# Attention with each head of a pair on its own 64 rows of the array, in packed banks

## What is computed

```python
q = (x @ wq).reshape(B, T, 32, 16); k = x @ wk; v = x @ wv
scores = einsum('bqhd,bkd->bhqk', q, k) / 4, causal
out = softmax(scores) @ v, heads side by side, @ wo
h = linear8bit(xn, W1, b1); g = silu(linear8bit(h, W2, b2))
return x + out * g
```

## Time and profile before

| | us |
|---|---|
| median of 3 runs | 799.04 (798.92 to 799.80) |
| profiled execution | 802.84, span 801.1 |
| PE busy | 764.9 (95%) |
| DVE busy | 638.7 (80%) |
| ACT busy | 402.7 (50%) |
| POOL busy | 257.6 (32%) |
| preparation | 0 to 81.3 |
| attention | 81.3 to 408.6 |
| the rest | 408.7 to 801.1 |

### The profile page before, as it was taken

The page is one execution under the profiler, slowest core; times in us unless marked ns, Lnnn a source line. Parts: engine busy times, 40 slices in busy tenths (PEclk is TensorE's granted clock), DMA queues, the critical chain, the costliest instruction groups (busy, mean ns, idle before and its releaser), DMA issues. The chain is left out here.

```text
span 801.1 us, 12089 instructions
## 1 busy us (share of the span) xinstructions
PE 764.9 (95%) x4253; PEld 579.5 (72%) x4253; DVE 638.7 (80%) x1094; ACT 402.7 (50%) x683; POOL 257.6 (32%) x335
## 2 busy tenths in 40 slices
PE   4999999999999999999999999999997999999995
PEld 3877665556676666775578888788886788888884
DVE  7988989999999899995537476666658998599957
ACT  3454166767677676777634554544553333122212
POOL 7313135555555555554621110110100000036504
PEclk9999589999999999999999999999999999999998
DMA  7421303333322223334554444222013778536982
GB/s 258 153 106 53 86 11 91 82 80 92 90 81 83 82 81 95 89 113 123 161 192 159 143 158 144 81 78 79 27 47 97 251 220 259 164 106 219 334 287 105
DMA packets 58348, 103.37 MB, mean 129 GB/s; under 512 B 8480, under 2 KB 16688, under 8 KB 56752
## 3 DMA queue, kind: packets, MB, share of 16 engines
q1 hardware_dynamic: 58288, 102.60, 40.3%
HBM read 52.76 MB, written 36.70 MB: 112 GB/s over the span
## 5 line engine op out<-in xcount | busy, mean ns | idle before, releaser
L914 DVE TENSOR_REDUCE rowmax<-ps 128x2 f32<-128x512 f32 (+3 forms) x384 | 210.9, 591 | 20.7 <-PE ps L991 18.8
L835 ACT ACTIVATE probs<-ps 128x512 f32<-128x512 f32 (+1 forms) x352 | 175.2, 557 | 72.4 <-PE ps L1004 70.7
L991 PE MATMUL ps<-km,stack 128*128 128x256 f32 (+3 forms) x512 | 151.0, 350 | 2.0 <-PEq L187 1.9
L1004 PE MATMUL ps<-stack,ks 128*128 128x512 f32 (+1 forms) x352 | 133.1, 388 | 2.6 <-ACT probs L835 2.6
L991 PEld LDWEIGHTS ps<-km,stack 128*128 128x128 f32 (+1 forms) x512 | 96.0, 201 | 42.2 <-DVE rowmax L914 22.5
L817 POOL TENSOR_SCALAR_AFFINE_SELECT probs<-probs 128x512 f32<-128x512 f32 x128 | 81.0, 641 | 79.1 <-ACT probs L835 77.6
L1806 PE MATMUL ps<-big_h 128*128 128x512 f32 x256 | 100.4, 392 | 2.4 <-issue 2.0
L1808 PE MATMUL ps<-big_h,big_l 128*128 128x512 f32 x256 | 100.3, 392 | 0.0
L1807 PE MATMUL ps<-big_l,big_h 128*128 128x512 f32 x256 | 100.2, 391 | 0.0
L1017 PE MATMUL ps<-probs,vones 128*32 128x512 f32 (+3 forms) x1024 | 82.2, 439 | 0.2 <-POOL probs L817 0.2
L1004 PEld LDWEIGHTS ps<-stack,ks 128*128 128x128 f32 x352 | 67.5, 192 | 11.9 <-ACT probs L835 6.3
(11 more groups left out here) (227 smaller groups left out, 1384.3 us busy)
## 6 DMA issues: line engine op xcount, KB each, us to landing
stack<-big_h SPq DMA_DIRECT2D x128, 64.0 KB, 2.0
h_scratch<-hs SPq DMA_DIRECT2D x7, 1024.0 KB, 4.5
hload<-h_scratch SPq DMA_DIRECT2D x14, 512.0 KB, 5.4
xn_scratch<-xa SPq DMA_DIRECT2D x4, 1024.0 KB, 4.4
stack<-big_l SPq DMA_DIRECT2D x64, 64.0 KB, 2.0
xi<-xn_scratch SPq DMA_DIRECT2D x16, 256.0 KB, 2.8
xe_scratch<-xm SPq DMA_DIRECT2D x16, 256.0 KB, 2.3
w2n<-in_L_ffn_W_dram SPq DMA_DIRECT2D x4, 1024.0 KB, 6.7
```

Of the source, the lines that this page charges most:

```text
L835: nc.scalar.activation(probs[p][:, o:o + nh * w], ps[:, STB[n % NST], 0:nh * w], ACT.Exp).then_inc(s_exp, 1)
L914: nc.vector.tensor_reduce(dst, src, AX_X, ALU.max).then_inc(s_red, 1)
L991: last = nc.tensor.matmul(dst, stack[u % 3][rows, hp, P * qt:P * (qt + 1)], km[rows, u // KT, p0:p0 + npar, keys], start=True, stop=True)
L1004: ins = nc.tensor.matmul(ps[:, STB[n % NST], 0:nh * w].rearrange("p (h q) -> p h q", h=nh), ks[:, u // KT, p, P * kt:P * (kt + 1)], stack[ ...
```

## The change

A head of a pair now has its own 64 rows of the stack: 48 rows of queries (high, low, high), two rows for the maximum, and a staircase of 14 rows with ten steps each (steps of 2^12). The keys need only one version each. What was a piece of two heads is now two products on rows 0-63 and 64-127, issued one after the other into two banks, and all banks are filled to 512 columns: 20 banks of maxima and 20 of scores per unit instead of 24 and 22, CH = 20, LAG = 10. The steps of everything else move along. A unit's queries are 24 DMAs of 16 rows, its maxima two DMAs. The values product of key tile 3 moves into the first group. The projection's rows are permuted by loading wo with eight DMAs. SP waits for the spare rows of a stack before the queries' DMAs, and no longer before the maxima's. POOL fills whole stacks, and adds the staircase to the keys. The wait for the last stores of projected rows moves from f = 1 to f = 0.

```diff
-SPARE, RUN, STEP = 100, 5, 2.0 ** 25
+SPARE, RUN, STEP, OWN = 50, 10, 2.0 ** 12, 32.0
...
-        km = sa("km", [P, B, 2, T], F32R)
-        ks = sa("ks", [P, B, 2, T], F32R)
+        km = sa("km", [P, B, T], F32R)
+        ks = sa("ks", [P, B, T], F32R)
...
+        HALF_ROWS, KEPT = P // 2, 3 * HD
         def fill_spare(i):
-            spare = slice(6 * HD, P)
-            return nc.gpsimd.tensor_copy(stack[i][spare, :, :].rearrange("r h (j k) -> r (h j) k", k=P),
-                                         later_q[spare, :].rearrange("r (o k) -> r o k", o=1)
-                                         .broadcast_to([P - 6 * HD, NPAIR * QT, P]))
+            return nc.gpsimd.tensor_copy(stack[i][:, :, :].rearrange("r h (j k) -> r (h j) k", k=P),
+                                         later_q[:, :].rearrange("r (o k) -> r o k", o=1)
+                                         .broadcast_to([P, NPAIR * QT, P]))
...
             for hp in range(NPAIR):
-                src = slice(2 * HD * hp, 2 * HD * (hp + 1))
-                for n, part in enumerate((big_h, big_l, big_h)):
-                    sp.dma_start(stack[u % 3][2 * HD * n:2 * HD * (n + 1), hp, :].bitcast(F32),
-                                 part[src, f, tok].bitcast(F32)).then_inc(s_sq[u % 3][hp], 16)
+                for a in range(2):
+                    src = slice(HD * (2 * hp + a), HD * (2 * hp + a + 1))
+                    for n, part in enumerate((big_h, big_l, big_h)):
+                        lo = HALF_ROWS * a + HD * n
+                        sp.dma_start(stack[u % 3][lo:lo + HD, hp, :].bitcast(F32),
+                                     part[src, f, tok].bitcast(F32)).then_inc(s_sq[u % 3][hp], 16)
...
-                            sp.dma_start(wo_in, wo.rearrange("(k p) n -> p k n", p=P)).then_inc(s_wload["wo"], 16)
+                            wo_rows = wo.rearrange("(k p) n -> p k n", p=P)
+                            for h2, h1, a in itertools.product(range(2), repeat=3):
+                                to, of = 2 * HD * (2 * h1 + a) + HD * h2, 2 * HD * (2 * h2 + h1) + HD * a
+                                sp.dma_start(wo_in[to:to + HD], wo_rows[of:of + HD]).then_inc(s_wload["wo"], 16)
...
+                        sp.wait_ge(s_z, 1)
                         stack_queries(sp, 0)
...
-                steps_along(later_k, [-STEP ** t for t in range(RUN + 1)])
                 fill_spare(0).then_inc(s_z, 1)
                 pool.wait_ge(s_z, 1)
+                steps_along(later_k, [-OWN * STEP ** t for t in range(RUN + 1)])
...
+                        step(nc.vector.tensor_scalar(ks[:, g, :], kvh, cols[:, 0:1], None, ALU.mult))
+                        ins = nc.vector.scalar_tensor_tensor(out=ks[:, g, :], in0=kvl, scalar=cols[:, 1:2],
+                                                             in1=ks[:, g, :].bitcast(F32),
+                                                             op0=ALU.mult, op1=ALU.add)
...
+        CH, NB = 20, 10
+        def pieces_of(c):
+            v, m = divmod(c // 2, 5)
+            hp = 2 * v + m // 2
+            if m == 4:
+                return [(2 * v + h, 1, own, 2 * P * h + P * own) for h in range(2) for own in (False, True)]
+            if m % 2:
+                return [(hp, 2, False, 0), (hp, 2, True, 2 * P), (hp, 0, True, 3 * P)]
+            return [(hp, 3, False, 0), (hp, 3, True, 3 * P)]
+        def scores_of(i):
+            return [[(0, 0, 1, 0)], [(0, 1, 1, 0)], [(1, 0, 1, 0), (3, 0, 1, 3 * P)],
+                    [(1, 1, 1, 0), (3, 1, 1, 3 * P)], [(2, 0, 2, 0)]][i]
+        def scores_at(i, a):
+            return ((0, 2 * T, OF_1, OF_1 + 2 * T, OF_2)[i]) + T * a
+        def probs_of(kt, j):
+            h, a = divmod(j, 2)
+            return {0: T * j, 1: OF_1 + T * j, 3: OF_1 + T * j + 3 * P, 2: OF_2 + T * a + 2 * P * h}[kt]
+        MASK_END = {4: (0,), 8: (1, 3), 10: (2,)}
+        MASK_OF = {0: 0, 1: 1, 3: 2, 2: 3}
+        GROUPS = [(0, 1, 3), (2,)]
...
-        LAG = 11
+        LAG = 10
         MAX_AT = 3
         STEPS = CH * (U + 3) + LAG
-        PV_AT = {11: (0, 0), 16: (0, 1), 22: (1, 0), 27: (1, 1)}
-        NORM_AT = {19: 0, 27: 1, 30: 2, 33: 3}
-        SHARE_AT, HIGH_AT, LOW_AT = 30, 34, 33
-        XLOAD_AT, XMASK_AT, XSCALE_AT, XROUND_AT, XBACK_AT, XSTORE_AT = -1, 15, 21, 25, 26, 30
+        PV_AT = {10: (0, 0), 14: (0, 1), 18: (1, 0), 22: (1, 1)}
+        NORM_AT = {16: 0, 24: 1, 26: 2, 29: 3}
+        SHARE_AT, HIGH_AT, LOW_AT = 25, 30, 29
+        XLOAD_AT, XMASK_AT, XSCALE_AT, XROUND_AT, XBACK_AT, XSTORE_AT = -1, 12, 16, 20, 22, 26
         T0 = 2 * CH + 4 - LAG
         def spread_over(windows):
             return {T0 + CH * w + at: (j, k) for j, (w, steps) in enumerate(windows) for k, at in enumerate(steps)}
-        EVENLY = (3, 7, 12, 16)
+        EVENLY = (3, 7, 10, 12)
...
                 def queries(u):
-                    if u >= 3:
+                    if u < 3:
+                        sp.wait_ge(s_z, u + 1)
+                    else:
                         sp.wait_ge(s_st, 2 * NB * (u - 2))
                     stack_queries(sp, u)
                 def maxima(u):
-                    if u < 3:
-                        sp.wait_ge(s_z, u + 1)
                     sp.wait_ge(s_mh, u + 1)
-                    sp.dma_start(stack[u % 3][6 * HD:6 * HD + 4, :, :].bitcast(F32),
-                                 mhl[:, :].bitcast(F32)).then_inc(s_sm[u % 3], 16)
+                    for a in range(2):
+                        lo = HALF_ROWS * a + KEPT
+                        sp.dma_start(stack[u % 3][lo:lo + 2, :, :].bitcast(F32),
+                                     mhl[HPF * a:HPF * (a + 1), :].bitcast(F32)).then_inc(s_sm[u % 3], 16)
...
+                        v, m = divmod(c // 2, 5)
                         if c == 0 and u >= 2:
                             dve.wait_ge(s_mf, misc_at[("m", u - 2, 0)] + 1)
                         dve.wait_ge(s_max, g + 1)
                         bank, mine = ps[:, MAXB[g % NMAX], :], rowmax[:, u % 2, :, :]
+                        of = NPAIR * (c % 2) + 2 * v
+                        if m == 4:
+                            src, dst = bank.rearrange("p (h k) -> p h k", h=2), mine[:, QT, of:of + 2]
+                        elif m % 2:
+                            src, dst = bank.rearrange("p (s k) -> p s k", k=P), mine[:, 0:QT, of + m // 2]
                         else:
+                            src, dst = bank, mine[:, QT + 2, of + m // 2:of + m // 2 + 1]
                         nc.vector.tensor_reduce(dst, src, AX_X, ALU.max).then_inc(s_red, 1)
                         if c == CH - 1:
                             dve.wait_ge(s_red, g + 1)
+                            nc.vector.tensor_reduce(mine[:, QT + 1, :], mine[:, 0:QT - 1, :].rearrange("p s h -> p h s"),
+                                                    AX_X, ALU.max).then_inc(s_rm, 1)
...
+                def max_pair(u, c):
                     n = CH * u + c
                     if c == 0 and u < 3:
                         pe.wait_ge(s_z, u + 1)
+                    if n + 1 >= NMAX:
+                        pe.wait_ge(s_red, n + 2 - NMAX)
+                    pieces = pieces_of(c)
+                    for hp, qt, own, at in pieces:
+                        pe.wait_ge(s_sq[u % 3][hp], 16 * 6 * (u // 3 + 1))
                         keys = slice(P * qt, P * qt + P) if own else slice(0, P * qt)
...
+                        for a in range(2):
+                            rows = slice(HALF_ROWS * a, HALF_ROWS * a + (HALF_ROWS if own else KEPT))
+                            dst = ps[:, MAXB[(n + a) % NMAX], at:at + keys.stop - keys.start]
+                            ins = nc.tensor.matmul(dst, stack[u % 3][rows, hp, P * qt:P * (qt + 1)],
+                                                   km[rows, u // KT, keys], start=True, stop=True)
+                            if (hp, qt, own, at) == pieces[-1]:
+                                ins.then_inc(s_max, 1)
+                def score_pair(u, s):
+                    p, i = divmod(s // 2, NB // 2)
                     n = 2 * NB * u + s
                     if s == 0:
+                        pe.wait_ge(s_sm[u % 3], 32 * (u // 3 + 1))
+                    if n + 1 >= NST:
+                        pe.wait_ge(s_exp, n + 2 - NST)
+                    parts = scores_of(i)
+                    for kt, h, nh, at in parts:
+                        w = T - P * kt
+                        for a in range(2):
+                            rows = slice(HALF_ROWS * a, HALF_ROWS * (a + 1))
+                            dst = ps[:, STB[(n + a) % NST], at:at + nh * w].rearrange("p (h q) -> p h q", h=nh)
+                            ins = nc.tensor.matmul(dst, ks[rows, u // KT, P * kt:P * (kt + 1)],
+                                                   stack[u % 3][rows, 2 * p + h:2 * p + h + nh, P * kt:T],
+                                                   start=True, stop=True)
```

(65 more changed lines are left out.)

121 lines of the change are left out of this document (40 added, 81 removed).

## The result

Before: 799.42 us, the median of 4 runs (798.92 to 801.68). After: **891.57 us**, the median of 4 (890.47 to 893.58). The ratio is 1.1149, 95% interval 1.1118 to 1.118: slower, as forecast, but by 92 us and not by 23, and outside the range of 787 to 842.

A forecast was written before the change was run, and what follows sets the result against it. After the change SP's issue queue was to bound the units: +15.5 us at the start, +11.9 over units 0 to 13, -2.7 in unit 14, -1.5 at the end, second stage 0: +23.2, giving 822 us, range 787 to 842.

The forecast's parts named there:

- TensorE was the bound before: Attention units of the kernel before: TensorE needs 17.65 of 18.30 us, with VectorE close behind.
- the halves run side by side: Paired 64-row products overlap fully, so a pair costs one product; maxima and scores fall from 9.4 to 6.0 us a unit.
- a free unit takes 17.15 us: Attention unit if only TensorE and VectorE counted: 17.15 us, 1.15 less than before.
- TensorE's 15.0 us: TensorE's work per attention unit after the change, including 0.8 us for changes between array shapes.
- 0.63 us for a copy of 16 rows: Issue of a query copy on SP's queue costs as much as a 32-row one; SP needs 18.0 us a unit.
- Rival B: A 16-row copy's issue on SP costs less than 0.63 us; at 0.47 us, about 789 us in all; chance 0.22.
- Rival C: Halves don't run side by side: a pair costs at least 0.22 us; 832 or about 850 us; chance 0.13.
- Start of the stage, +15.5: First score product of unit 0 comes 15.5 us later, behind 48 query copies and the maxima's DMA.
- Who waits for SP: SP's program-order queue delays the maxima's DMA, which scores two units on await: 18.95 us per unit instead of 18.30.
- The two-unit chain, 18.95 us: From first score product of unit w to that of w+2, through SP's queue and maxima: 37.9 us, 18.95 a unit.
- Unit 14 and the tail, -4.2: Unit 14, with no queries behind it, takes 19.0 us (-2.7); last unit and end save 1.5 us.
- Second stage, 0: Stage after attention: only a wait moves from second to first block; 0 us, at most 0.5.

The follow-up runs named there:

- experiment 6: Kernel after with 6 query copies of 64 rows: 855.24 us; with 12 of 32 rows: 812.14 us. Kernel before with 3 of 128 rows: 815.45 us.
- the kernel of twelve: Kernel after with 12 query copies of 32 rows a unit, two pairs in each, instead of 24 of 16 rows: 812.14 us.
- experiment 8: Kernel after with 12 query copies, plus overwritten products where TensorE idles: 798.66 us. Control, kernel before with such products at its start: 800.22 us.
- experiment 1: Kernel before with each 32-row query copy cut in two of 16 rows, 24 issues a unit, no halves: 901.04 us, ratio 1.1267.
- experiment 2: Kernel after with two tiles xm used in turn, so POOL's mask waits for the store before last: 874.19 us (855.21 to 878.52).
- experiment 4: Kernel after with 20 overwritten products a unit ahead of the second set's value products, where TensorE waited: 902.71 us, ratio 1.1279.
- experiment 5: Kernel after with two tiles xm, plus overwritten products ahead of each unit's first scores: 847.78 us with 8 products, 849.02 us with 5.

## Why the prediction was wrong, step by step

**TensorE was the bound before; the halves run side by side; a free unit takes 17.15 us.** The result is right. In the kernel after, the two products of a pair start 3 ns apart (259.307 and 259.310 us), and the free unit is the 17.34 us of experiment 6. VectorE's 16.45 us a unit came out at 16.47, its stalls of 0.7 at 0.87. TensorE's 15.0 us was too low: in the later units of the kernel of twelve it is busy 16.84 us a unit. From start to start in one of them (208.15 to 225.48) the score products take 3.9 us and not 2.6, the maxima products 4.0 and not 3.4, the projections 3.6 and not 2.8; that is 2.6 us more than their bare prices, where 0.8 had been put down for all changes of shape. A pair of 512 columns, for one, takes 0.38 us to the product of another shape behind it (208.15 to 208.53) and not 0.24. That the free unit came out all the same is luck in part: TensorE's own need stayed 0.5 us under the 17.34.

**0.63 us for a copy of 16 rows.** Right: 0.59 and 0.04. Rival B fell with that. Rival C fell with the 3 ns and with the free unit: four pairs of 128 columns take 0.50 us (214.06 to 214.56 in the kernel of twelve), 0.13 a pair and not the 0.22 of rival C.

**Start of the stage, +15.5.** +18.0: the right size. The preparation did not get 1.0 us shorter: its last part became 1.1 us longer (first maxima product at 82.65 instead of 81.53). The copies took 31.3 us and not 30.2, and from the first of the two maxima DMAs to the first score product it was 3.06 us (115.69 to 118.75) and not 0.75 + 3.04. The queue was not all that could hold the start. In the kernel of twelve, whose copies end at 102.95, the first exponential still comes 9.3 us later than before. Of these, 3.6 lie ahead of the first maxima product (85.15 against 81.53), and 3.8 between it and the transposes of unit 0's maxima (18.3 us against 14.5), where a pair of banks takes 1.6 us (0.80 for TensorE at half clock, then 0.78 of waiting for VectorE). With the clock at 1.00 (experiment 8), 2.0 of the 9.3 are gone.

**"Who waits for SP": this step failed.** It followed the maxima's DMA, which gives 18.95 us a unit, and of the store of xe it said only where it stands in the queue and that it costs 0.62 us. Who waits for that store was never asked. The ring through it is 0.8 (L738 to xi) + 0.4 + 15.2 + 2.4 (issue to landing) + 1.3 (POOL's mask) + 2.5 (three reductions between L727 and L738) = 22.6, and 23.3 to 23.8 with the issues that now and then take longer (1.89 us at 267.21). Experiments 1, 2 and 4 show it: with 24 issues and no halves it is there, with a second tile it is gone, and at full clock it is as long. The trace of before held all that was needed to price it. The store was issued 7.9 us behind xi (226.86 to 234.76), and POOL and VectorE took the tile up like this:

```profile
237.58 1.28 POOL L785 TENSOR_TENSOR xm<-xi,inlier_row 128x512 f32<-128x512 f32 x1
...
241.57 0.67 DVE L704 TENSOR_REDUCE xs<-xm 128x1 f32<-128x512 f32 x1
...
244.39 0.74 DVE L715 SCALAR_TENSOR_TENSOR xm<-xi,xs,magic_row 128x512 f32<-128x512 f32 x1
```

The mask ends at 238.86 and VectorE takes its result at 241.57, 2.7 us later; over units 1 to 13 it is 1.8 to 2.9 us. That was the ring's slack in a unit of 18.3. An estimate from these rows: 18.3 less 1.8 to 2.9, plus 7.6 for 12 more issues, gives 23.0 to 24.1 us a unit, against the 23.4 measured. The waits of the kernel before had a hint that I did not use:

```profile
POOL xm L785 <- DMA xe_scratch<-xm: 4.3, 7, 0.8
```

Seven times POOL already waited for that store, by up to 0.8 us. That was not yet a loss, since VectorE came later still in all units but one, but it named the store as what POOL's mask waited for.

**The two-unit chain, 18.95 us.** Right as a chain, 18.84 to 19.07 at full clock in experiment 5, but it would not have been the time even without the ring. It leaves TensorE idle some 3 us in two units, and behind such a wait the clock stood at 0.50 for 16 us (experiment 2). Every duration that I added up was one of clock 1.00. This second term, 855 to 879 us in experiment 2 where the sum would have said about 831, was in no rival.

**Unit 14 and the tail, -4.2.** Measured -1.4; unit 14 took 20.5 us (first exponentials 444.19 to 464.67) and not 19.0. What holds it was not tested. **Second stage, 0:** -1.5.

Open: why the clock after a wait of 2.2 us in experiment 6 came back in 3.7 us, and after 3.1 us in experiment 2 and 1.6 us in experiment 5 only in 16. The runs show that added work can prevent the fall, not what ends it.

## What to carry to other kernels

When a change lengthens a queue, list every entry behind the lengthened part, and for each one who waits for it, until the chain closes on itself; the ring with the longest period sets the pace, and it may cross engines that look idle. Then take the slack of each ring from the trace of before, by how long each result lies there before it is used: what is added beyond the slack is paid in full (here 5.1 of 7.6 us a unit). A wait that occurs in the trace of before, even by tenths of a microsecond, marks a place to look at first. And price a new wait on TensorE with the work behind it at half clock. Filling the idle time with products that nobody reads took 13 us off the kernel of twelve and 7 to 31 off the one with two tiles xm; it gave nothing in the kernel before, and cost 11 in the kernel after, where another ring set the pace.

## What the runs showed of the hardware

- The issue of a copy on SP's queue took 0.59 + 0.04 us for 16, 32 and 64 rows of 2 KB alike, and 0.61 + 0.04 for 128. Moving 128 KB in one copy took 4.7 us to land, 32 KB 2.0 us (medians). Fewer, larger copies freed the queue and came later (experiment 6).
- Products on rows 0-63 and 64-127 run side by side whether or not they stand in turn in the program (812.14 and 811.94 us; starts 3 and 10 ns apart).
- A unit with less work on TensorE took longer (19.5 us against 17.34 in one and the same trace), because the granted clock was 0.80 and not 1.00: with added products and the clock at 1.00 the same units took 17.33 us (experiment 8).
